# Attention in a post-norm block: for the maxima of the first and last query blocks the causal mask is added by VectorE instead of by mask products

## The reference, cut to what matters

```
x: (8, 512, 256)                                     # B, T, C
attention: 16 heads of 16, each projected to a latent of 32 with rotary embedding
  att = einsum('bhql,bhkl->bhqk', q_for_k, k_lat) * L ** (-0.5)
  att = where(causal, att, -inf);  att = softmax(att, axis=-1)
  y_lat = einsum('bhqk,bhkl->bhql', att, v_lat);  y = y_lat @ l2o_w.T + l2o_b
x = layernorm(x + y @ cproj_w.T + cproj_b)
feed-forward: soft mixture of 16 experts with 64 slots each
  logits = layernorm(x) . slots;  dispatch = softmax over tokens;  combine = softmax over slots
  out = combine @ (down(gelu(gate) * up))
x = layernorm(x + out)
```

## Time and profile before

| | |
|---|---|
| three runs | 1233.32, 1235.87, 1236.91 us |
| the profiled execution | 1233.49 us |
| its span | 1231.8 us |
| mean granted TensorE clock | 0.983 of 2.4 GHz |
| TensorE busy | 96% of the span |
| VectorE, ScalarE, GpSimd busy | 63%, 55%, 36% |

### The profile page before, as it was taken

How to read it: one execution, slowest core, us unless ns; L and a number is a source line. 1 busy time by engine, 2 the same in 40 slices (tenths; PEclk the granted TensorE clock), 3 DMA queues, 4 the chain that set the end, 5 groups by cost and what they waited for, 6 DMA issues and landing times.

```text
span 1231.8 us, 19727 instructions
## 1 busy us (share of the span) xinstructions
PE 1183.5 (96%) x7126; PEld 932.5 (76%) x7126; DVE 780.0 (63%) x1330; ACT 673.2 (55%) x1042; POOL 448.2 (36%) x336
## 2 busy tenths in 40 slices
PE   6799999999999999997999999999999999999996
PEld 5566766666666666665888888877888888889885
DVE  6767787868686868765577777765454445432444
ACT  3545456565746465648687777756455555430112
POOL 6455565565645555511100000003544444430000
PEclk8799999999999999998999999999999999999999
DMA  4644545454555363710233335337555555364671
GB/s 144 142 113 113 138 95 128 126 132 126 138 129 148 91 163 83 207 62 36 89 123 114 120 121 180 103 120 245 157 162 167 171 179 179 111 210 132 233 248 54
DMA packets 126672, 170.32 MB, mean 138 GB/s; under 512 B 47041, under 2 KB 77186, under 8 KB 126594
## 3 DMA queue, kind: packets, MB, share of 16 engines
q1 hardware_dynamic: 124498, 168.74, 47.0%
q10 hardware_dynamic: 2096, 0.56, 0.2%
HBM read 72.26 MB, written 37.75 MB: 89 GB/s over the span
## 4 chain that ended last, share of the span: by engine, by line
PE 84%; DVE 7%; ACT 5%; DMA 1%; issue 1%; POOL 1%; SPq 1%; ACTq 0%; DVEq 0%; POOLq 0%
PE ring L414 11%; PE ring L416 10%; PE ring L415 10%; PE ring L1367 7%; PE ring L1511 7%; PE ring L1352 6%; PE tail L1378 6%; PE tail L414 3%; PE tail L416 3%; PE tail L415 3%; PE tail L1338 2%; PE ring L1354 2%; PE ring L1400 2%; PE tail L1511 2%; ACT x L825 2%; PE ring L1436 2%
## 5 line engine op out<-in xcount | busy, mean ns | idle before, releaser
L1079 DVE TENSOR_REDUCE mx<-ring 128x4 f32<-128x512 f32 (+2 forms) x192 | 200.5, 1046 | 88.7 <-PE ring L1354 88.2
L806 ACT ACTIVATE pt<-ring 128x1024 f32<-128x1024 f32 (+1 forms) x192 | 168.9, 881 | 100.3 <-PE ring L1367 76.0
L684 POOL TENSOR_SCALAR_AFFINE_SELECT pt<-pt 128x512 f32<-128x512 f32 x128 | 84.8, 663 | 194.4 <-ACT pt L806 193.9
L1352 PE MATMUL ring<-qks 96*128 96x384 f32 (+3 forms) x512 | 141.5, 365 | 7.7 <-DMA qks<-stg 3.6
L1367 PE MATMUL ring<-qks 98*128 98x256 f32 (+3 forms) x512 | 138.0, 373 | 8.6 <-DVE mx L1079 4.7
L1367 PEld LDWEIGHTS ring<-qks 98*128 98x128 f32 x512 | 78.6, 192 | 75.1 <-issue 38.7
L709 POOL TENSOR_TENSOR hl<-hid,hh 128x512 fp32r<-128x512 f32 x64 | 82.6, 1301 | 78.3 <-ACT hh L901 78.3
L1352 PEld LDWEIGHTS ring<-qks 96*128 96x128 f32 x512 | 92.0, 198 | 15.2 <-issue 5.1
L1188 DVE SCALAR_TENSOR_TENSOR hid<-ring,bias_e,gate 128x512 f32<-128x512 f32 x64 | 47.8, 748 | 80.9 <-ACT gate L895 47.2
L1378 PE MATMUL tail<-pt,va 128*32 128x512 f32 (+3 forms) x1024 | 95.9, 447 | 2.1 <-POOL pt L684 2.1
L1354 PE MATMUL ring<-maskb,identb 128*128 128x128 bf16 (+2 forms) x352 | 91.4, 260 | 0.0
(11 more groups left out here) (227 smaller groups left out, 3071.6 us busy)
## 6 DMA issues: line engine op xcount, KB each, us to landing
qks<-stg SPq DMA_DIRECT2D x384, 128.0 KB, 2.4
c_dram<-c2s SPq DMA_DIRECT2D x32, 512.0 KB, 4.9
c<-c_dram SPq DMA_DIRECT2D x32, 512.0 KB, 6.2
sl_dram<-sls SPq DMA_DIRECT2D x32, 256.0 KB, 3.4
wg<-in_wg SPq DMA_DIRECT2D x16, 512.0 KB, 5.6
wu<-in_wu SPq DMA_DIRECT2D x16, 512.0 KB, 6.5
wd<-in_wd SPq DMA_DIRECT2D x16, 512.0 KB, 7.1
sl<-sl_dram SPq DMA_DIRECT2D x16, 512.0 KB, 4.5
```

The source lines that it names most:

```text
L684: nc.gpsimd.affine_select(out=m, in_=m, compare_op=ALU.is_ge, fill=0.0, base=0, pattern=[[0, GH], [1, P]], channel_multiplier=-1).then_inc ...
L806: nc.scalar.activation(pt[j % 2][:, h:h + heads, 0:n], heads_of(tile, heads, n), ACT.Exp, scale=SCALE).then_inc(empty, 1)
L1079: nc.vector.tensor_reduce(out=mx[:, g, h:h + heads, i], in_=heads_of(tile, heads, (i + 1) * P), axis=AX.X, op=ALU.max).then_inc(empty, 1)
L1352: nc.tensor.matmul(scores[:, h, :], qks[0:KS_ROWS, g, 0, h0 + h, i * P:(i + 1) * P], qks[0:KS_ROWS, g, 1, h0 + h, 0:n], start=(h == k), st ...
```

## The change

`MASK_ADDED` names query blocks 0 and 3. For these, TensorE issues no mask product, and each head's product opens and closes its own accumulation. VectorE runs, instead of one reduction a unit, one `tensor_tensor_reduce` for each head: it adds a float32 mask (`maskf`, 0 or the -1e30 triangle in its last 128 columns) to the scores in place, in PSUM, and its accumulator output is the maximum. `maskf` is made at the step `slotg` by a memset and a copy of `maskb`. Blocks 1 and 2 stay as they were. All hand-set positions are new, and with them the order of the steps on all five engines.

```diff
+LOWEST = -3e38
+MASK_ADDED = (0, 3,)
...
-PE_AT = {"lat": -20.75, "wqk": -9.0, "max": 0.0, "neg": 10.5, "exp": 12.75, "v": 13.55, "pv": 15.0, "yT": 27.75, "yTT": 55.5, "cproj": 57.5, "wv": -12.2, "seT": 6}
-ACT_AT = {"xth": -44.5, "lat": -22.0, "khi": -11.6, "qhi": -9.6, "neg": 8.82, "exp": 11.74, "y": 21.75, "yTT": 54.85, "apply": 75.0, "wlat": -30, "senorm": -2, "seT": 7, "seh": 7.1}
-DVE_AT = {"xtl": -33.0, "blat": -28.9, "kvrows": -28.8, "slotg": -28.75, "shuffle": -20.8, "cos": -16.0, "qlo": -10.5, "max": -2.36, "negmax": 5.8, "v": 11.0, "yT": 25.9, "cproj": 56.1, "ln": 56.5, "wlat": -29, "wv": -15.75, "sestat": -15.85, "sescale": -7.95, "sel": 8.5}
-POOL_AT = {"sin": -27.31, "add": -23.69, "klo": -21.17, "mask": 1.94, "bias": 41.5}
-SP_AT = {"xt": -66.0, "x": 31.25, "stack": -19.9, "store": 89.0}
+PE_AT = {"lat": -21.25, "wqk": -9.75, "max": 0.5, "neg": 10.0, "exp": 12.0, "v": 13.55, "pv": 14.5, "yT": 27.0, "yTT": 53.5, "cproj": 57.0, "wv": -12.2, "seT": 6}
+ACT_AT = {"xth": -44.75, "lat": -20.0, "khi": -9.1, "qhi": -8.35, "neg": 9.82, "exp": 12.24, "y": 21.25, "yTT": 53.85, "apply": 78.75, "wlat": -30, "senorm": -2, "seT": 7, "seh": 7.1}
+DVE_AT = {"xtl": -31.25, "blat": -28.9, "kvrows": -28.8, "slotg": -28.75, "shuffle": -21.3, "cos": -17.25, "qlo": -10.0, "max": -1.36, "negmax": 6.55, "v": 11.75, "yT": 24.9, "cproj": 55.6, "ln": 56.0, "wlat": -29, "wv": -17.0, "sestat": -17.1, "sescale": -9.2, "sel": 8.5}
+POOL_AT = {"sin": -26.06, "add": -24.69, "klo": -21.17, "mask": -1.06, "bias": 32.5}
+SP_AT = {"xt": -44.75, "x": 40.75, "stack": -3.15, "store": 99.5}
...
-PE_JOIN = (55, 28, 28, 23, 23, 18, 18, 18, 17, 17, 14, 12, 12, 12, 5, 3, 3, 1, 1)
+PE_JOIN = (55, 36, 31, 24, 23, 21, 21, 19, 17, 17, 14, 12, 12, 12, 3, 3, 1)
...
-    at[0] += 3 * KB
+    maskf = place("maskf", [P, T], f32)
+    at[0] += KB
...
                 elif name == "slotg":
+                    nc.vector.memset(maskf[:, 0:T - P], 0.0).then_inc(mask_made, 1)
+                    dve.wait_ge(pool_ready, MASKB_POOL)
+                    nc.vector.tensor_copy(maskf[:, T - P:T], maskb[:, 0, :]).then_inc(mask_made, 1)
...
                     i, h, heads = MAX_UNITS[st[3]]
+                    scores = heads_of(tile, heads, (i + 1) * P)
+                    if (b, g, st[3]) == (0, 0, 0):
+                        dve.wait_ge(mask_made, 2)
                     dve.wait_ge(full, fill_count(st))
-                    nc.vector.tensor_reduce(out=mx[:, g, h:h + heads, i], in_=heads_of(tile, heads, (i + 1) * P), axis=AX.X,
-                                            op=ALU.max).then_inc(empty, 1)
+                    if i in MASK_ADDED:
+                        for k in range(heads):
+                            last = nc.vector.tensor_tensor_reduce(out=scores[:, k, :], in0=scores[:, k, :], in1=maskf[:, (NT - 1 - i) * P:T], scale=1.0,
+                                                                  scalar=LOWEST, op0=ALU.add, op1=ALU.max, accum_out=mx[:, g, h + k, i:i + 1])
+                    else:
+                        last = nc.vector.tensor_reduce(out=mx[:, g, h:h + heads, i], in_=scores, axis=AX.X, op=ALU.max)
+                    last.then_inc(empty, 1)
...
                         for h in range(k, k + some):
-                            nc.tensor.matmul(scores[:, h, :], qks[0:KS_ROWS, g, 0, h0 + h, i * P:(i + 1) * P],
-                                             qks[0:KS_ROWS, g, 1, h0 + h, 0:n], start=(h == k), stop=False)
-                        last = nc.tensor.matmul(scores[:, k:k + some, i * P:n], identb[:, :], maskb[:, 0:some, :], start=False, stop=True)
+                            last = nc.tensor.matmul(scores[:, h, :], qks[0:KS_ROWS, g, 0, h0 + h, i * P:(i + 1) * P],
+                                             qks[0:KS_ROWS, g, 1, h0 + h, 0:n], start=(h == k or i in MASK_ADDED), stop=(i in MASK_ADDED))
+                        if i not in MASK_ADDED:
+                            last = nc.tensor.matmul(scores[:, k:k + some, i * P:n], identb[:, :], maskb[:, 0:some, :], start=False, stop=True)
```

More of the change, by code:

```diff
@@ L114 @@
            ("c2", 0, 0), ("c2", 0, 1), ("c2", 0, 2), ("c2", 0, 3), ("slots", 0, 1))
-PE_JOIN = (55, 28, 28, 23, 23, 18, 18, 18, 17, 17, 14, 12, 12, 12, 5, 3, 3, 1, 1)
-ACT_JOIN = (29, 23, 18, 18, 15, 14, 12, 12, 12, 11, 10, 10, 9, 9, 8, 8, 3, 2, 1, 1, 1, 1, 1, 1, 1, 1, 1, 1, 1, 1, 1, 1, 1, 1)
-DVE_JOIN = (21, 16, 9, 8, 6, 6, 5, 5, 5, 5, 5, 5, 5, 5, 5, 5, 5, 4, 4, 3, 3, 2, 2, 2, 1)
-SP_JOIN = (6, 5, 2, 2, 1, 1, 1, 1, 1, 1)
+PE_JOIN = (55, 36, 31, 24, 23, 21, 21, 19, 17, 17, 14, 12, 12, 12, 3, 3, 1)
+ACT_JOIN = (28, 22, 20, 19, 15, 15, 14, 12, 11, 11, 11, 10, 8, 8, 8, 8, 2, 1, 1, 1, 1, 1, 1, 1, 1, 1, 1, 1, 1, 1, 1, 1, 1, 1)
+DVE_JOIN = (21, 16, 12, 11, 7, 6, 6, 5, 5, 5, 4, 4, 4, 4, 4, 4, 4, 4, 4, 2, 2, 2)
+SP_JOIN = (5, 4, 2, 2, 1, 1, 1, 1, 1, 1, 1)
 PAIR_STEPS = ("lat", "max", "exp", "v", "yTT", "cproj", "wv", "seT", "zT", "s1", "s2", "d", "c2", "slots")
@@ L318, in block_kernel @@
     se_normed, se_high, se_ready = sem("se_normed"), sem("se_high"), sem("se_ready")
-    pool_ready = sem("pool_ready")
+    pool_ready, mask_made = sem("pool_ready"), sem("mask_made")
     setup_dve = sem("setup_dve")
@@ L386, in block_kernel @@
     SE_DVE = WV_DVE + 2 + 3 * NEWTON + 1
-    POOL_SETUP = 10
+    MASKB_POOL, POOL_SETUP = 8, 10
     IN_LAT, IN_SMALL, IN_ROPE, IN_SG, IN_SE, IN_TAIL = 5, 7, 2, 3, 1, 4
@@ L643, in _ @@
                                     pattern=[[0, GH], [-1, P]], channel_multiplier=1).then_inc(pool_ready, 1)
-            pool.wait_ge(pool_ready, 8)
+            pool.wait_ge(pool_ready, MASKB_POOL)
             nc.gpsimd.memset(va[:, :, :, HD:L], 1.0).then_inc(pool_ready, 1)
```

## The result

The changed kernel takes 1258.47 us, median of 4 runs (1257.1 to 1262.12), against 1234.8 us for the kernel before on the same chip: ratio 1.0195 with a 95% interval of 1.0167 to 1.0223: slower, clear of the noise, by about 2%. The profiled execution took 1259.14 us (span 1257.4, before 1231.8).

What follows compares the result with a forecast made beforehand. TensorE, busy 96%, was taken as the bound: 1233.49 us minus 12.3 for mask products plus 2 for waits is 1223.2; with 2.4 from profiled run to median 1225.6, say 1225. Own range 1215 to 1233, with rivals 1213 to 1243.

Steps and rivals of the forecast that it cites:

- The mask products: TensorE, blocks 0 and 3: removal gains 0.44 us a group, 14.1 us in 32 groups, 12.3 of it in time.
- VectorE's price: New operations on VectorE: 0.68 us for 512 elements, 0.28 for 128; rival, whole durations plus a read: 1270, chance 0.20.
- The strict rule: VectorE: the next operation does not start until the pipeline is empty; by it the time would be about 1270.
- Whether the buffers come back: Score buffers between TensorE and VectorE: VectorE's 7.1 us just fits in TensorE's 7.3 us.
- The place where a batch stalls: Layer norm on VectorE: GpSimd's addition should be over by then; TensorE stall of 0.5 us (0 to 1.7).
- The rival for this place: Layer norm: L1116 meets GpSimd's sin, 1.7 us instead of 0.8 in 8 batches: 1233; chance 0.18 shared with The order alone.
- The join: Last batch meeting the expert routing: could go either way, 4.6 us each way, put at nothing.
- The order alone: New order without the operation gains at most 0.8 us a batch: 1230; chance 0.18 shared with The rival for this place.

Runs made afterwards that it cites:

- run 11: run 6's kernel with no new operation, all mask products back: 1242.88 us, ratio 1.0064 against the kernel before.
- run 6: run 4's kernel with GpSimd's sin product and addition each as two instructions of 512 elements: 1229.18 us, ratio 0.9961 against the kernel before.
- after: The changed kernel itself, with the new operation for blocks 0 and 3 and all new orders: 1258.47 us, ratio 1.0195 against the kernel before.
- run 1: after without the new operation, all mask products back, new orders kept: 1272.57 us, ratio 1.0302 against the kernel before.
- run 9: after with GpSimd's sin product and addition on 8 elements only, the other elements' rotation left out: 1213.3 us, ratio 0.982 against the kernel before.
- run 4: after with GpSimd's sin and addition moved ahead of the mask that the last exponential releases: 1234.7 us, ratio 0.9986 against the kernel before.
- run 8: run 4's kernel with the four join orders of the kernel before: 1250.86 us, ratio 1.0105 against the kernel before.

## Why the prediction was wrong, step by step

**The mask products** held in their sum: 14.1 us of TensorE were predicted for 32 groups, and 0.47 a group, 15, are in the timelines of runs 11 and 6. In time the prediction counted 12.3 of them, less 2 for new waits; the runs gave 14.1 (after against run 1) and 13.7 (run 6 against run 11), 3 to 4 more. Their split did not hold: block 3 was put at 0.20 a group (0.16 to 0.40) and is 0.42. The step compared its masked unit (0.67) with an exponential's unit (0.57); its own kind without masks takes 0.46. Block 0 was put at 0.24 and is 0.05 in the new order: in run 11 the next product starts 0.04 us after its one mask product. Two errors of a fifth of a microsecond cancelled, which was luck.

**VectorE's price** held: 0.68 and 0.28 taken, 0.65 and 0.25 measured, the accumulator worth 0.05 instead of 0.08. VectorE's busy time in a batch of run 6 is 54.16 us, predicted 53.5, but that agreement is luck: 2.7 of it are cos, held by sin. In run 9, where next to nothing is held, it is 50.49. The strict rule of the Trainium skill's page "VectorE: DVE Perf Modes", section "The DRAIN you can't avoid", is not borne out here: successors start 0.65 us after an operation recorded for 0.76. The section itself adds that a next operation that is not held starts earlier, and that is what the trace shows. What the page's section "Two Vector instructions with no wait between them" says, that an accumulator output makes two instructions, the trace shows (256 reads of 141 ns).

**Whether the buffers come back** held: in a group without a norm TensorE waits for no maximum.

**The place where a batch stalls** is the step that failed: "GpSimd's addition is now ahead of the masks, right behind cos, and should be over by then". It was derived from where the addition stands relative to cos, and GpSimd takes its steps in order. Sin, which the addition needs, stands behind a mask that waits for the group's last exponential (288.06), and both then run from 289.33 to 294.16, over the norm. A stall of 0.5 us was predicted, 3.75 came, and 1.76 at the lower clock behind it, which no case had. The rival for this place had the right mechanism, sin meeting the norm, but let one operation be held, once (1.7 us): 1233. The prediction's own sum with 3.75 + 1.76 instead of 0.8 in the six batches that stall gives 1225.6 + 28.3 = 1254, far beyond the top of its range. Of the 33.5 us between forecast and result the five middle batches alone make up 27 (68.33 instead of about 62.9).

**The join** with the routing was put at nothing, 4.6 us each way. It was mis-sized: in run 11, without operation and long stall, the stretch behind the fifth middle batch takes 8.8 us more than before. The 4.5 us between 1254 and the result lie there or in the order's small waits; the runs don't divide them.

The Trainium skill has the rule on its page "SBUF — State Buffer", section "Who interferes with whom": VectorE and GpSimd share one pair of ports, an operation that needs it holds it for its whole length and the other waits. It counts copies and tensor-scalar operations in SBUF among VectorE's, and those with two inputs in SBUF, and leaves reductions out. The trace agrees (2.18 and 2.34 us held; the reduction at 360.72 in run 4, beside a mask on GpSimd, takes its usual 1.21). By this rule the norm's cost turns on where sin and the addition lie in time; that question the prediction answered from the order's table alone.

**The order alone** as a rival was put at 1230, "no more than the 0.8 us a batch": it bounded what an order can gain, and not what it can lose. It is 1272.57.

Open: the rest of what run 8 loses beside its wait of 7.8 us, what of run 9's 45 us is the shorter chain, and 0.5 to 0.7 us of what a batch of after loses. No run tried a version with the norm's small operations moved instead of sin.

## What to carry to other kernels

When an order is moved by hand, don't read the new place of an instruction from its table alone: for each in-order queue find what the instruction in front of it waits for, and put its time against everything that excludes it on another engine. A short operation on SBUF that met a long one of GpSimd cost the long one's remaining time here, so count such meetings one by one; the operations that took their scores from PSUM were free of it. And a stall of some microseconds on TensorE is to be priced with the slow clock behind it: 3.75 us cost another 1.8 here. When an order is changed together with an operation, run the order without the operation too: here that showed 37 us that no average of busy time had shown.

## What the runs showed of the hardware that was not expected

- An operation of VectorE on 4 elements in SBUF takes 0.17 us alone and 2.18 us behind the start of a GpSimd product of 2.38 us; cos takes 3.06 instead of 1.23. Each GpSimd instruction holds one operation: two whole ones held 2.18 and 2.34, four halves held 1.08 to 1.19 each.
- It works the other way round: a mask on GpSimd took 1.62 instead of 0.64 us beside cos. New operations on scores in PSUM took 0.34 us beside sin, 0.33 without it.
- After a stall of 3.75 us TensorE's granted clock was 0.53 for 4.97 us, then 1.00; after one of 0.79 us it stayed at 1.00.
- A bf16 product of 512 columns between units of small float products cost TensorE 0.05 us, although it is recorded for 0.39; four products of 128 columns cost 0.42.
